# Three stacked graph attention layers on one Trainium2 core: score columns formed on VectorE, the first loads put in another order, ones multiplied on TensorE, and a new order for the first and last six turns

## The chip, the cores and the metric

The kernel runs on one core of one Trainium2 chip. The metric is the device time in microseconds (us) of one execution; of several executions the median is taken. The engines of the core are TensorE (PE in the rows), VectorE (DVE), ScalarE (ACT), GpSimd (POOL) and SyncE (SP), which here only issues transfers. Each engine works through its own instructions in order and waits for the others by semaphores.

## What is computed

There are 32 independent graphs of 256 nodes, with 256 float32 features each (`x`), and a 0/1 adjacency (`adj`, int32). Every layer projects the features, forms one score for each pair of nodes from two vectors of attention weights, masks it by the adjacency, takes a softmax, and averages the projected features with it:

```python
Wh = x @ W                                   # layer A: one head of 256
e = leaky_relu((Wh @ a1)[:, :, None] + (Wh @ a2)[:, None, :], 0.2)
h = elu(softmax(where(adj == 0, -1e9, e), axis=2) @ Wh)
x = layernorm(x + h)
# layer B: 4 heads of 128, softmax over the sources, mask adj > 0 or diagonal, + b1, elu
# layer C: input 512 wide, 1 head of 256, + b2
x = layernorm(x + layerC(elu(layerB(x))))
```

## The kernel before

One graph is one **turn** (32 in all, b0 to b5 for the first six, e6 to e1 for the last six). A turn passes through layer A (project, softmax, weigh, residual, layernorm), then B with four heads, then C. Several turns are in work at once, each at another stage. On every engine the order is written out by hand as three lists: `fill` (the first six turns), `body` (repeated 25 times, one full turn of work) and `drain` (the last six). Within a list a call such as `maxima(A, 0, 3, b0)` names layer, head or tile, the PSUM bank, and the turn.

A score of a projected row is the row times an attention vector. The kernel obtains it from the projection itself, by two more weight columns in front of W (columns 0 and 1 of `WA`, `WB`, `WC`), which hold W times the two attention vectors, scaled by 0.8 and -0.8. Before, TensorE makes these columns at the start: the transposed weights (`WTA`, `WTB`, `WTC`) are loaded as well, `scale_vectors` (L841) scales the vectors on VectorE, `score_products` (L1422) multiplies in pieces of two columns, and `score_columns` (L848) copies the sums into W. The first projection waits for that copy (`pe.wait_ge(A.s_wab, 1)` in `project_a`, L1457).

Weights of B and C are used as a rounded high part and a low part: `round_weights` on ScalarE waits for the score columns, and `split_weights` on VectorE for the rounding. The steps of one turn of layer A, which the first turn must pass through before B can begin, are: `project_a` (L1465, PE), `values` (ACT), `spread` (L1494, PE: scores laid out along rows), `maxima`, `top`, `logit`, `shift` (DVE), `exp` (ACT), `transpose_weights` (L1505, PE), `weights_copy` (ACT), `weigh` (L1513, PE), `inverse_sum` (L951, DVE), `norm_first`, `elu_exp_first` (ACT), `elu_first` (L963, DVE), `residual` (POOL), `stats`, `meanvar` (L1031, DVE), `rstd`, `normalise` (POOL), and `transpose_x1` (L1534, PE), with which the input of B is made. `column_sums` and `spread_b1` make the bias terms on TensorE, once. In C the last turn has the same steps, then `norm_last`, `stats`, `meanvar` and `normalise`, and a store.

`warm_up(b, count)` (L1455) multiplies a square of ones by itself count times; its result is not read. A float32 matmul of the program is two instructions in the trace.

Of the kernel before, what the change touches and what calls it, by code (L numbers as in the profile page):

```python
# [11 lines left out]
P = 128  # L12
# [37 lines left out]
def gat_kernel(nc, x, xT, adj, adjT, w0, w0T, w1, w1T, w2, w2T, vectors, biases, out):  # L50
# [13 lines left out]
    B = Layer("B", w1.shape[1] // P, P, D // P)  # L64
# [6 lines left out]
    with ctx:  # L71
# [15 lines left out]
        vec = sb("vec", [P, 2 * (D // P + B.H + D // P)])  # L87
# [4 lines left out]
        for L in LAYERS:  # L92
            L.W = sb("W" + L.name, [P, L.KT, L.H, L.F + 2])
            L.WT = sb("WT" + L.name, [P, L.H * L.F // P, L.KT * P])
# [11 lines left out]
        for L in LAYERS:  # L106
# [31 lines left out]
        s_cst, s_cst2, s_vec, s_rows, s_vecs, s_b1r, s_b1z, s_b1x, s_cs, s_b2 = (sem(n) for n in (  # L138
            "constants", "identity_made", "vectors_loaded", "biases_loaded", "vectors_scaled", "b1_spread", "b1_zeros", "b1_made",
            "column_sums", "b2_made"))  # L140
        for L in LAYERS:
            L.s_wld, L.s_wtld, L.s_wa, L.s_wab, L.s_round, L.s_split = (
                sem(k + L.name) for k in ("weights_loaded_", "weights_T_loaded_", "score_products_", "score_columns_",
                                          "weights_rounded_", "weights_split_"))
# [59 lines left out]
        def load_weights_T(eng, L):  # L204
            wT = w0T if L is A else w1T if L is B else w2T
            eng.dma_start(L.WT[:, :, :], wT.rearrange("(q p) k -> p q k", p=P)).then_inc(L.s_wtld, DMA)

        def load_vectors(eng):
            eng.dma_start(vec[:, :], vectors).then_inc(s_vec, DMA)
# [7 lines left out]
        def _(sp):  # L217
# [30 lines left out]
            def fill():  # L248
                b0, b1, b2, b3, b4, b5 = Turn(0), Turn(1), Turn(2), Turn(3), Turn(4), Turn(5)
                load_weights(sp, A)  # L250
                load_adj(b0)
                load_xT(b0)
                load_xT(b1)
                load_weights_T(sp, C)
                load_weights(sp, B)
                load_adj(b1)
                load_adjT(b0)
                load_residual(b0)
                load_weights(sp, C)
                load_adj(b2)  # L260
                load_adj(b3)
                load_residual(b1)
                load_xT(b2)
                load_adjT(b1)
                load_adjT(b2)
                load_residual(b2)
                load_adj(b4)
                load_adjT(b3)
                load_xT(b3)
                load_adjT(b4)  # L270
                load_xT(b4)
# [3 lines left out]
                store(b0)  # L275
                load_xT(b5)
                load_residual(b5)

# [8 lines left out]
            def drain():  # L287
                e6, e5, e4, e3, e2, e1 = Turn(NB - 6), Turn(NB - 5), Turn(NB - 4), Turn(NB - 3), Turn(NB - 2), Turn(NB - 1)
                load_xT(e1)
# [1516 lines left out]
```

## Time and profile before

| | |
|---|---|
| median of 3 runs | 669.05 us (668.47 to 672.19) |
| the profiled execution | 667.11 us, of which the profiled span is 665.2 us |
| TensorE busy | 637.9 us, 96% of the span |
| VectorE busy | 588.7 us, 88% |
| ScalarE busy | 482.0 us, 72% |
| GpSimd busy | 448.6 us, 67% |
| matmuls, weight loads | 4156 of each |

The page cuts the span into 40 slices. TensorE is at 90% or more of all slices but the first four and the last; the granted clock of TensorE is full in all but the last. Busy time is counted in microseconds of occupation, whatever the clock: a matmul at half the clock counts double. Where a row gives idle time in brackets, the name behind the arrow is what the engine had waited for.

### The profile page before, as it was taken

To read this page: it belongs to the slowest core of one execution; us is meant where nothing else is said; L and a number is where in the kernel's file an instruction comes from. 1 tells how busy PE (TensorE), PEld (TensorE's weight loads), DVE (VectorE), ACT (ScalarE), POOL (GpSimd) and SP (SyncE) were. 2 spreads that over 40 slices of the span, in tenths; PEclk is the share of its full clock that TensorE was granted. 3 is DMA by queue.
4 is the path that set the end of the run, shared out by engine and by line. 5 is a ranking of instruction groups with operands and counts; after the bars stand their busy time and mean duration, and the time that the engine had idled before them with its cause. 6 is when DMAs were issued, how large, how long until landed. Compare 5 with 4: busy or idle time off the path is not lost. (4 is left out here: it accounts for less than half of the span.)

```text
span 665.2 us, 17485 instructions
## 1 busy us (share of the span) xinstructions
PE 637.9 (96%) x4156; PEld 574.9 (86%) x4156; DVE 588.7 (88%) x2315; ACT 482.0 (72%) x1220; POOL 448.6 (67%) x811
## 2 busy tenths in 40 slices
PE   6979999999999999999999999999999999999993
PEld 5758899998999999999999989999999999988871
DVE  1488999999999999999999999999999999899953
ACT  1457887787778777777787777778877777687661
POOL 0247577777777777677777777777777777666762
PEclk9999999999999999999999999999999999999996
DMA  8311112222212222221122222211222222210001
GB/s 269 96 48 36 46 49 80 81 65 81 67 37 75 81 81 80 65 81 62 40 77 81 81 67 78 81 48 50 80 81 80 65 80 73 89 33 0 18 17 47
DMA packets 46693, 45.68 MB, mean 69 GB/s; under 512 B 2817, under 2 KB 46337, under 8 KB 46594
## 3 DMA queue, kind: packets, MB, share of 16 engines
q1 hardware_dynamic: 45648, 43.79, 20.8%
q8 instruction: 35, 0.57, 0.4%
q10 hardware_dynamic: 946, 0.80, 0.4%
q14 instruction: 64, 0.52, 0.3%
HBM read 36.19 MB, written 8.39 MB: 67 GB/s over the span
## 5 line engine op out<-in xcount | busy, mean ns | idle before, releaser
L378 POOL TENSOR_SCALAR probB<-probB,rdenB 128x256 f32<-128x256 f32 x256 | 124.7, 499 | 79.9 <-DVE rdenB L958 79.6
L558 ACT ACTIVATE probB<-probB,shiftB 128x256 f32<-128x256 f32 x256 | 127.1, 499 | 16.8 <-DVE shiftB L927 13.0
L1524 PE MATMUL PS<-probTB,VB 128*128 128x256 f32 x512 | 128.2, 382 | 0.9 <-ACT probTB L577 0.8
L941 DVE SCALAR_TENSOR_TENSOR probB<-PS,VB,gatedB 128x256 f32<-128x256 f32 x256 | 111.5, 478 | 1.8 <-issue 0.4
L389 POOL TENSOR_TENSOR inlC<-hidT,inhC 128x512 fp32r<-128x512 f32 x64 | 82.0, 1281 | 43.7 <-ACT inhC L622 43.6
L899 DVE CUSTOM_DVE_ANT_0 gatedB<-PS,gate_bc 128x256 f32<-128x256 f32 x256 | 93.8, 420 | 7.3 <-PE PS L1494 5.5
L1524 PEld LDWEIGHTS PS<-probTB,VB 128*128 128x128 f32 x512 | 89.3, 190 | 11.0 <-ACT probTB L577 2.1
L1480 PE MATMUL PS<-WhB,inhB 128*128 128x260 f32 x256 | 81.8, 319 | 1.4 <-DVE inlB L972 1.2
L577 ACT ACTIVATE probTB<-PS 128x512 f32<-128x512 f32 x128 | 72.9, 591 | 9.9 <-PE PS L1505 9.6
L360 POOL TENSOR_TENSOR y<-y,xres 128x512 f32<-128x512 f32 x32 | 41.1, 1286 | 52.4 <-DVE y L963 52.4
L1480 PE MATMUL PS<-WhC,inhC 128*128 128x258 f32 x256 | 75.4, 294 | 0.5 <-issue 0.4
L1505 PE MATMUL PS<-ident,probB 128*128 128x128 f32 x512 | 72.4, 273 | 1.4 <-POOL probB L378 1.4
L1480 PE MATMUL PS<-WlC,inhC 128*128 128x258 f32 x256 | 72.5, 283 | 0.0
L1480 PE MATMUL PS<-WhB,inlB 128*128 128x260 f32 x256 | 72.5, 283 | 0.0
L1480 PE MATMUL PS<-WlB,inhB 128*128 128x260 f32 x256 | 72.3, 282 | 0.0
L1480 PE MATMUL PS<-WhC,inlC 128*128 128x258 f32 x256 | 72.3, 282 | 0.0
L1513 PE MATMUL PS<-VC,probTC 128*128 128x257 f32 x256 | 67.3, 389 | 1.7 <-ACT probTC L577 1.7
L1465 PE MATMUL PS<-WA,xTin 128*128 128x258 f32 x256 | 65.4, 397 | 0.3 <-issue 0.3
L1513 PE MATMUL PS<-VA,probTA 128*128 128x257 f32 x256 | 64.7, 393 | 0.0
L1505 PEld LDWEIGHTS PS<-ident,probB 128*128 128x128 f32 x512 | 59.6, 141 | 5.5 <-issue 2.4
L611 ACT ACTIVATE ehid<-PS,minus 128x512 f32<-128x512 f32 x64 | 44.0, 687 | 28.1 <-issue 17.2
L987 DVE TENSOR_TENSOR VB<-PS,b1x 128x260 f32<-128x260 f32 x128 | 54.2, 426 | 10.6 <-PE PS L1480 9.2
(108 smaller groups left out, 1626.1 us busy)
## 6 DMA issues: line engine op xcount, KB each, us to landing
adj_in<-in_adj_dram SPq DMA_DIRECT2D x32, 256.0 KB, 4.3
xTin<-in_x_t_dram SPq DMA_DIRECT2D x32, 256.0 KB, 4.1
adjT_in<-in_adj_t_dram SPq DMA_DIRECT2D x32, 256.0 KB, 3.1
xres<-in_x_dram SPq DMA_DIRECT2D x32, 256.0 KB, 2.8
out_dram<-res SPq DMA_DIRECT2D x32, 256.0 KB, 2.1
WTC<-in_L_gnn_W_t_dram SPq DMA_DIRECT2D x1, 512.0 KB, 7.4
WTB<-in_L_gnn_W_t_dram ACTq DMA_DIRECT2D x1, 512.0 KB, 8.0
WB<-in_L_gnn_W_dram SPq DMA_DIRECT2D x2, 256.0 KB, 8.3
```

The lines of the kernel that those rows point to most:

```text
L378: last = pool.tensor_scalar(B.prob[h][:, k, :], B.prob[h][:, k, :], B.rden[:, k, h:h + 1], 1.0, ALU.mult, ALU.mult)
L389: pool.tensor_tensor(C.inl[:, s, :], hidT[:, s, :], C.inh[:, s, :].bitcast(F32), ALU.subtract)\
L558: last = nc.scalar.activation(L.prob[h][:, k, :], L.prob[h][:, k, :], ACT.Exp, bias=L.shift[:, k, h:h + 1], accum_out=den[:, k, h:h + 1] i ...
L577: nc.scalar.activation(L.probT[h][:, :, :], PS[b][:, :].rearrange("p (k n) -> p k n", k=NT), ACT.Copy)\
L899: last = nc.vector.tensor_tensor_reduce(out=L.gated[h][:, k, :], in0=PS[b][:, (h % 2) * N:(h % 2 + 1) * N], in1=gate[:, k, :], scale=0.25, ...
L941: last = nc.vector.scalar_tensor_tensor(out=L.prob[h][:, k, :], in0=PS[b][:, (h % 2) * N:(h % 2 + 1) * N], scalar=L.V[:, k, h, 1:2], in1=L ...
L987: nc.vector.tensor_tensor(B.V[:, tile, hs, :], PS[b][:, 0:2 * (B.F + 2)].rearrange("p (h f) -> p h f", h=2), b1x[:, hs, :], ALU.add).then_ ...
L1465: last = nc.tensor.matmul(PS[b][:, 0:D + 2], xTin[t.at % 2][:, k, tile * P:(tile + 1) * P], A.W[:, k, 0, :], start=(k == 0), stop=(k == A. ...
L1480: last = nc.tensor.matmul(PS[b][:, 0:n * (L.F + 2)], x_[:, k, tile * P:(tile + 1) * P], w_[:, k, n * g:n * (g + 1), :].rearrange("p h f -> ...
L1505: last = nc.tensor.transpose(PS[b][:, o:o + P], L.prob[h][:, q, k * P:(k + 1) * P], ident[:, :])
L1513: last = nc.tensor.matmul(PS[b][:, 0:L.F + 1], L.probT[0][:, k, u * P:(u + 1) * P], L.V[:, k, 0, 2:L.F + 3], start=(k == 0), stop=(k == NT ...
L1524: last = nc.tensor.matmul(PS[b][:, o:o + N], B.V[:, k, h, 2:B.F + 2], B.probT[h][:, k, :], start=(k == 0), stop=(k == NT - 1))
```

## The change

1. **Score columns.** `score_products`, `scale_vectors` and the loads of the transposed weights are gone. The attention vectors are loaded spread over all 128 partitions (`attA`, `attB`, `attC`), and VectorE multiplies each row of W by them and sums along the row, one instruction for each k, head and vector: 4 for A and 8 for C (256 columns), 16 for B (128 columns).
2. **Loads.** SyncE issues A's weights and the first xT, then waits until A's weights have landed, and issues the rest after that, adjacencies of b0 first. ScalarE issues A's vectors and the biases, waits for A's weights too, and issues the vectors of B and C. TensorE and ScalarE no longer wait for the identity at the start; the first `spread` does.
3. **Ones.** TensorE multiplies ones 11 times at the start (4 before), 6 times behind the first `spread`, 4 times behind the first `weigh`, and 12 times behind the last `spread`.
4. **Order.** `fill` and `drain` of all five engines are new lists of the same calls. `body` is the same.

```diff
+        def load_vectors(eng, L):
+            if L is A:
+                eng.dma_start(A.att[:, :, :], a0.rearrange("(j f) o -> j (f o)", j=2).partition_broadcast(P))\
+                    .then_inc(A.s_attld, DMA)
+            else:
+                for j, v in enumerate((asrc1, adst1) if L is B else (asrc2, adst2)):
+                    eng.dma_start(L.att[:, j, :], v.rearrange("h f -> (h f)").partition_broadcast(P))\
+                        .then_inc(L.s_attld, DMA)
...
                 load_weights(sp, A)
+                load_xT(b0)
+                sp.wait_ge(A.s_wld, DMA)
                 load_adj(b0)
-                load_xT(b0)
+                load_adjT(b0)
+                load_weights(sp, B)
+                load_weights(sp, C)
                 load_xT(b1)
-                load_weights_T(sp, C)
-                load_weights(sp, B)
                 load_adj(b1)
...
             def round_weights(L):
                 act.wait_ge(L.s_wld, (B.KT if L is B else 1) * DMA)
-                act.wait_ge(L.s_wab, 1)
+                act.wait_ge(L.s_wab, 2 * L.KT * L.H)
...
-                load_weights_T(act, A)
-                load_vectors(act)
+                load_vectors(act, A)
+                load_biases(act)
+                act.wait_ge(A.s_wld, DMA)
+                load_vectors(act, B)
+                load_vectors(act, C)
                 load_table()
...
+            def score_columns(L, k, heads):
+                dve.wait_ge(L.s_wld, (B.KT if L is B else 1) * DMA)
+                dve.wait_ge(L.s_attld, (1 if L is A else 2) * DMA)
+                for h in heads:
+                    for j in range(2):
+                        v = L.att[:, 1 - j if L is A else j, h * L.F:(h + 1) * L.F]
+                        if L.columns > 1:
+                            dve.wait_ge(L.s_wab, L.columns - 1)
+                        nc.vector.scalar_tensor_tensor(out=L.prod[:, j, :], in0=L.W[:, k, h, 2:L.F + 2],
+                                                       scalar=0.8 if j == 0 else -0.8, in1=v, op0=ALU.mult, op1=ALU.mult,
+                                                       accum_out=L.W[:, k, h, j:j + 1]).then_inc(L.s_wab, 1)
+                        L.columns += 1
...
                     if t.first:
                         pe.wait_ge(A.s_wld, DMA)
-                        pe.wait_ge(A.s_wab, 1)
+                        pe.wait_ge(A.s_wab, 2 * A.KT)
...
-                warm_up(7, 4)
-                score_products(A, 6)
-                project_a(1, 0, b0)
+                warm_up(0, 11)
+                project_a(0, 7, b0)
```

VectorE, the start of `fill`, before: two scaled vectors, then the softmax of b0, and the copies of C's and B's columns behind it.

```order
L874 TENSOR_SCALAR gate_a<-adj_in 128x512
L845 TENSOR_SCALAR vec<-vec 128x8 x2
L850 COPY WA<-PS 128x2x2
...
L927 SCALAR_TENSOR_TENSOR shiftA<-topA,amaxA 128x2
L951 RECIPROCAL rdenA<-PS 128x1 x2
L874 TENSOR_SCALAR gate_a<-adj_in 128x512
L850 COPY WC<-PS 128x4x2
L850 COPY WB<-PS 128x8x2
L883 TENSOR_SCALAR gate_bc<-adjT_in 128x512
L963 SCALAR_TENSOR_TENSOR y<-e,y 128x512
```

The same place now; `prod` takes the products, which nothing reads, and the sums go to W.

```order
L851 SCALAR_TENSOR_TENSOR prodA,WA<-WA,attA 128x256 x4
L877 TENSOR_SCALAR gate_a<-adj_in 128x512
...
L930 SCALAR_TENSOR_TENSOR shiftA<-topA,amaxA 128x2
L851 SCALAR_TENSOR_TENSOR prodB,WB<-WB,attB 128x128 x16
L851 SCALAR_TENSOR_TENSOR prodC,WC<-WC,attC 128x256 x2
L954 RECIPROCAL rdenA<-PS 128x1 x2
L877 TENSOR_SCALAR gate_a<-adj_in 128x512
L858 TENSOR_TENSOR WlB<-WB,WhB 128x1040
L851 SCALAR_TENSOR_TENSOR prodC,WC<-WC,attC 128x256 x2
L966 SCALAR_TENSOR_TENSOR y<-e,y 128x512
L851 SCALAR_TENSOR_TENSOR prodC,WC<-WC,attC 128x256 x4
L1024 BN_STATS statA<-y 128x6 x2
```

Eighteen products now stand between the first turn's shift and its reciprocals, two and the split of B's weights between these and its elu, and four between elu and statistics.

TensorE at the very start, before.

```order
L1455 MATMUL PS<-ones 128x128 x4
L1432 MATMUL PS<-vec,WTA 128x2 x4
L1465 MATMUL PS<-WA,xTin 128x258 x4
L1494 MATMUL PS<-ident,VA 128x128 x2
L1432 MATMUL PS<-vec,WTC 128x2 x8
L1505 MATMUL PS<-ident,probA 128x128 x4
L1465 MATMUL PS<-WA,xTin 128x258 x2
L1513 MATMUL PS<-VA,probTA 128x257 x4
L1432 MATMUL PS<-vec,WTB 128x2 x8
```

And now.

```order
L1450 MATMUL PS<-ones 128x128 x11
L1460 MATMUL PS<-WA,xTin 128x258 x4
L1491 MATMUL PS<-ident,VA 128x128 x2
L1450 MATMUL PS<-ones 128x128 x6
L1502 MATMUL PS<-ident,probA 128x128 x4
L1510 MATMUL PS<-VA,probTA 128x257 x4
L1450 MATMUL PS<-ones 128x128 x4
L1460 MATMUL PS<-WA,xTin 128x258 x2
```

The two-column products are gone, ones stand in their places, and the second turn's first projection has moved behind the first turn's weighing.

GpSimd, the last turns of `drain`, before: the correction of C's scores for the last turn (`VC<-VC,fix`) stands ahead of the layernorm of the turn before it.

```order
L389 TENSOR_TENSOR inlC<-hidT,inhC 128x512 x2
L336 TENSOR_SCALAR veC<-mvC 128x2
L337 TENSOR_SCALAR nmC<-mvC 128x2
L339 TENSOR_TENSOR rstdC<-veC,power 128x2
L352 TENSOR_SCALAR res<-y,nmC,rstdC 128x256 x2
L370 TENSOR_TENSOR x1b<-x,b2x 128x512
L399 TENSOR_SCALAR VC<-VC,fix 128x2
L336 TENSOR_SCALAR veC<-mvC 128x2
```

And now.

```order
L392 TENSOR_TENSOR inlC<-hidT,inhC 128x512
L355 TENSOR_SCALAR res<-y,nmC,rstdC 128x256 x2
L392 TENSOR_TENSOR inlC<-hidT,inhC 128x512
L339 TENSOR_SCALAR veC<-mvC 128x2
L340 TENSOR_SCALAR nmC<-mvC 128x2
L342 TENSOR_TENSOR rstdC<-veC,power 128x2
L355 TENSOR_SCALAR res<-y,nmC,rstdC 128x256 x2
L402 TENSOR_SCALAR VC<-VC,fix 128x2
```

One normalisation has moved between the two low parts that the last projection of C waits for, and the next turn's layernorm ahead of the last correction; on TensorE the 12 multiplications of ones stand there between the last spread and the transposes behind it.

## Rows read from the trace of the kernel before

**Rows 1.** The page's first part: busy us and share of the span.
```profile
PE 637.9 (96%) x4156; PEld 574.9 (86%) x4156; DVE 588.7 (88%) x2315; ACT 482.0 (72%) x1220; POOL 448.6 (67%) x811
```

**Rows 2.** Busy time by stretch: length, each engine, clock, DMA share, GB/s.
```profile
0.00:9.76 9.76, 3.92 (x16) 3.60 (x17) 0.90 (x5) 1.49 (x2) 1.07 (x11) 1.00 0.77 245
9.76:21.64 11.88, 11.40 (x37) 9.53 (x38) 1.84 (x8) 2.28 (x5) 0.00 (x0) 1.00 0.59 175
21.64:31.12 9.48, 8.06 (x41) 5.48 (x40) 5.39 (x21) 4.38 (x8) 3.48 (x7) 1.00 0.54 168
31.12:35.30 4.18, 4.18 (x19) 3.80 (x20) 2.88 (x6) 1.19 (x2) 2.51 (x4) 0.59 0.07 10
35.30:50.41 15.11, 10.41 (x61) 7.90 (x61) 13.44 (x51) 9.02 (x24) 6.72 (x13) 1.00 0.16 50
50.41:86.84 36.43, 36.35 (x240) 32.00 (x241) 32.00 (x127) 27.75 (x74) 23.99 (x42) 1.00 0.12 38
105.84:583.86 478.02, 477.27 (x3197) 437.88 (x3196) 454.90 (x1796) 372.48 (x946) 349.26 (x625) 1.00 0.23 71
640.00:665.20 25.20, 12.38 (x58) 8.99 (x56) 9.42 (x32) 6.04 (x13) 10.43 (x20) 0.76 0.12 42
```

**Rows 3.** The same of L1432 alone: length, PE, PEld, clock, DMA share, GB/s.
```profile
0.00:31.12 31.12, 7.12 (x40) 7.26 (x40) 1.00 0.63 195
```

**Rows 4.** Timeline of the start: start, duration, engine, line, instruction, idle before.
```profile
0.78 0.44 SPq L202 DMA_DIRECT2D WA<-in_L_gnn_W_dram  x1
2.05 2.05 PE L1455 MATMUL PS<-ones 128*128 128x128 f32 x8 [2.05 <-POOL ident L316]
7.29 0.24 DVE L845 TENSOR_SCALAR vec<-vec 128x8 f32<-128x8 f32 x2 [2.55 <-DMA vec<-in_vectors_dram]
...
9.76 3.78 PE L1465 MATMUL PS<-WA,xTin 128*128 128x258 f32 x8 [0.30 <-issue]
```

**Rows 5.** DMA issues of the first 60 us: size, median us to landing.
```profile
WB<-in_L_gnn_W_dram SPq DMA_DIRECT2D x2, 256.0 KB, 8.3
WC<-in_L_gnn_W_dram SPq DMA_DIRECT2D x1, 512.0 KB, 8.2
WA<-in_L_gnn_W_dram SPq DMA_DIRECT2D x1, 256.0 KB, 2.8
```

**Rows 6.** Timeline of the first turn's way to layer B; the last is turn b3's.
```profile
14.02 0.69 PE L1494 MATMUL PS<-ident,VA 128*128 128x128 f32 x2 [0.48 <-ACT VA L548]
17.88 1.08 PE L1505 MATMUL PS<-ident,probA 128*128 128x128 f32 x4
...
22.13 0.17 DVE L951 RECIPROCAL rdenA<-PS 128x1 f32<-128x1 f32 x1 [5.39 <-PE PS L1513]
25.10 0.69 DVE L963 SCALAR_TENSOR_TENSOR y<-e,y 128x512 f32<-128x512 f32 x1
28.22 0.25 DVE L1031 BATCH_NORM_AGGREGATE mvA<-statA 128x2 f32<-128x6 f32 x2
31.12 0.66 PE L1534 MATMUL PS<-ident,x 128*128 128x128 f32 x4 [0.89 <-POOL x L352]
...
86.84 0.61 PE L1534 MATMUL PS<-ident,x 128*128 128x128 f32 x4
```

**Rows 7.** Lines L963, L916 and L899 on VectorE: least, median and most ns.
```profile
L963 DVE SCALAR_TENSOR_TENSOR y<-e,y x32: 671/673/693, 25.1 to 612.5; 128x512 f32<-128x512 f32 x32
...
L916 DVE SCALAR_TENSOR_TENSOR topC<-amaxC,VC x32: 144/161/164, 68.2 to 650.5; 128x2 f32<-128x2 f32 x32
...
L899 DVE DVE_READ_ACCUMULATOR2_ANT amaxA<- x64: 81/83/88, 15.2 to 600.3; 128x1 f32 x64
```

**Rows 8.** Timeline of the end, behind the last projection of C.
```profile
649.16 0.40 PE L1494 MATMUL PS<-ident,VC 128*128 128x128 f32 x2 [0.57 <-ACT VC L548]
652.81 0.82 PE L1505 MATMUL PS<-ident,probC 128*128 128x128 f32 x4 [3.24 <-ACT probC L558]
654.40 3.77 PE L1513 MATMUL PS<-VC,probTC 128*128 128x257 f32 x8 [0.78 <-ACT probTC L577]
```

More of the change, by code:

```diff
@@ L1076, in fill @@
+                maxima(B, 1, 5, b0)
+                inverse_sum_head(3, b0)
+                top(B, 0, b0)
+                logit(B, 0, 5, b0)
+                shift(B, 0, b0)
+                elu_first(b1)
+                logit(B, 1, 5, b0)
+                inverse_sum_head(0, b0)
+                stats(A, b1)
+                meanvar(A, b1)
+                elu(1, 3, b0)
                 maxima(A, 0, 1, b2)
-                elu_first(b1)
+                make_gate_b(b2)
+                logit(A, 0, 1, b2)
@@ L1230, in drain @@
                 maxima(B, 3, 2, e4)
[L1231 to L1241 removed]
+                logit(B, 2, 2, e4)
+                top(B, 1, e4)
@@ L1242, in drain @@
+                elu(0, 6, e5)
+                shift(B, 1, e4)
+                values_b(1, 0, 0, e4)
+                make_gate_a(e2)
+                inverse_sum(A, 0, 5, e3)
+                values_b(0, 0, 4, e4)
+                logit(B, 3, 2, e4)
+                inverse_sum(A, 1, 3, e3)
+                maxima(B, 0, 1, e4)
+                inverse_sum_head(2, e4)
+                maxima(B, 1, 1, e4)
+                logit(B, 0, 1, e4)
+                top(B, 0, e4)
                 elu_first(e3)
-                maxima(B, 1, 5, e4)
@@ L1279, in drain @@
+                elu(0, 6, e4)
+                logit(B, 3, 3, e3)
+                shift(B, 1, e3)
+                values_b(1, 0, 7, e3)
+                values_b(0, 0, 2, e3)
+                inverse_sum(A, 0, 0, e2)
                 make_gate_a(e1)
-                logit(B, 3, 5, e3)
+                maxima(B, 1, 4, e3)
+                maxima(B, 0, 4, e3)
+                inverse_sum_head(2, e3)
+                top(B, 0, e3)
                 elu_first(e2)
-                shift(B, 1, e3)
-                values_b(1, 0, 0, e3)
@@ L1321, in drain @@
+                shift(C, 0, e4)
+                values_b(0, 1, 6, e2)
+                shift(A, 0, e1)
+                make_gate_b(e1)
+                elu(1, 2, e3)
+                values_b(1, 1, 7, e2)
+                maxima(B, 2, 7, e2)
+                logit(B, 2, 7, e2)
+                maxima(B, 3, 7, e2)
+                values_b(0, 0, 0, e2)
                 top(B, 1, e2)
+                values_b(1, 0, 3, e2)
+                elu(0, 4, e3)
                 shift(B, 1, e2)
-                elu_first(e1)
@@ L1400, in drain @@
+                shift(C, 0, e1)
+                inverse_sum(C, 0, 7, e1)
+                norm_last(0, 7, e1)
+                inverse_sum(C, 1, 0, e1)
+                norm_last(1, 0, e1)
                 stats(C, e1)
@@ L1488, in spread @@
                     take_bank(b, L.s_logit[2 * g:2 * g + 2], t)
+                    if t.first:
+                        pe.wait_ge(s_cst2, 1)
                     for tile in range(NT):
```

1149 lines of the change are left out of this document (538 added, 611 removed).

## The prediction

> **What bounds the kernel now.** I read the busy times first: TensorE is busy for 637.9 of 665.2 us [rows 1], and in the stretch of the full turns it is idle for 0.75 us of 478.0 [rows 2]. These turns stay as they are, so they can give nothing. What is left is the start and the end, read from the stretches [rows 2] and then from the timelines [rows 4, 6, 8].
>
> As the end of the start I take turn b3's transposes of x1 at 86.84 [rows 6]; TensorE has the same calls ahead of them in both lists, but for the score products and the ones. The start loses time in four ways:
> - the first projection runs at 9.76, behind a wait for the vectors (scaled from 7.29 on) and the products for A [rows 4];
> - the first turn's chain through layer A goes on to 31.12 [rows 6]. From 9.76 to 31.12 TensorE is idle for only 1.9 us [rows 2], but of its 23.4 busy us ahead of 31.12 the two-column products are 7.1 [rows 2, 3], and the durations show half the clock (1.2 GHz) up to about 21.6: four transposes take 1.08 us at 17.88 and 0.61 at 86.84 [rows 6]. The clock column says 1.00 there; the durations decide;
> - right after 31.12 there is a stretch at a granted clock of 0.59, 4.18 us of which about 3.4 lie at 1.2 GHz. That costs 1.7 us;
> - from 35.30 to 50.41 TensorE is idle for 4.7 us while VectorE is busy for 13.44 of 15.11 [rows 2].
>
> At the end, everything behind the last spread (649.16) is one chain of the last turn, 16.0 us to the end of the span. TensorE waits 3.24 us in it, and its last eight matmuls take 3.77 us [rows 8] in a stretch whose mean granted clock is 0.76 [rows 2].
>
> **The change part by part: the start.** I walk the first turn through the new lists, on the clock of the span.
>
> *First projection.* A's weights are issued at 0.78 and land 2.8 us later [rows 4, 5], so at 3.6. No row of before shows a load spread over the partitions; it lies between 3.6 (as A's weights) and 7.3 (when the small vector load was usable [rows 4]). I take 4.0, since it is now issued at once and little is in flight beside it. Then four products of 256 columns. The same instruction form on two SBUF operands takes 673 ns for 512 columns and 161 for 2 [rows 7], so 1.0 ns a column: 0.42 us for 256, 0.29 for 128. The read of the accumulator (83 ns) may lie beside the next one or come on top: 0.35 to 0.50, and 0.22 to 0.37. I take 0.43 and 0.29, with the operand form that is closest. The columns are ready at 4.0 + 1.7 = 5.7. TensorE is in its ones: 4 took 2.05 us [rows 4], so 11 take up to 5.6 from 1.5 on (the wait for the identity is gone), and the next matmul can start at about 6.6. So **6.6 for 9.76**; with vectors at 7.3 it is 9.0.
>
> *To the transposes.* From first projection to spread it took 4.26 us (9.76 to 14.02), of it 3.78 matmuls at half the clock. Eleven matmuls of full width and the projections then run back to back, so I take full clock (2.4 GHz) for most of it: 2.5 us, spread at 9.1 (at half the clock 10.9). Spread to transposes took 3.86, all of it the VectorE and ScalarE chain: now 3.6, transposes at 12.7. The six ones behind the spread take 1.7 us (3.1 at half the clock) inside that wait, so they are hidden either way. Gates of the first turn need adjacencies issued at about 3.7 and 4.2; at 2.8 us each, as A's weights, they are there before 9.1.
>
> *To the reciprocals.* The copy takes 0.6 and a latency; weighing starts at 13.95 and its first half could be inverted at 15.1. But VectorE's queue is in order, and between the shift (done at 11.5) and the reciprocals stand 16 products for B and 2 for C: 16 x 0.29 + 2 x 0.43 = 5.5. **The reciprocals come at 17.0** for 22.13 before, 1.9 later than the data (bounds 15.8 and 18.4). What is behind them waits as well: the rounding of B's weights, then the first turn's norms on ScalarE.
>
> *To x1.* Reciprocal to elu took 2.97 (22.13 to 25.10), and does so again, with the split of B's weights and two products inside it: elu at 20.0. Elu to the end of the aggregation took 3.37 (25.10 to 28.47); four products for C now fit beside the residual on GpSimd but for 0.1 to 0.4: 23.5. From there to x1 it took 2.65: **x1 at 26.1 for 31.12, 5.0 earlier**, with bounds of 23.5 and 29.5 from the ends above. Score products for C and B on TensorE lay beside this chain or delayed it; they are in the difference already. The bias matmuls fit into TensorE's idle time ahead of 26.1.
>
> *From x1 to b3.* Before, 31.12 to 86.84 held 50.9 us of busy time and 4.8 idle [rows 2]. The same calls at full clock are 49.2. The idle time does not shrink, since the first two turns must still go through VectorE, ScalarE and GpSimd one behind the other, and they start closer together with less TensorE work between them. Walking the heads of b0 I find waits of about 0.8, 1.9, 1.0, 0.7 and 1.7 us up to the second x1, and then little. I take 7.0 in all, between 4.8 (as before) and 10. The full turns are reached at 26.1 + 49.2 + 7.0 = 82.3 for 86.84: **4.5 us gained**; bounds about -1 and 9.
>
> **The end.** The same calls stand in other places. TensorE is idle for little ahead of the last projection, and that one is bound by the chain elu, high part, low part of the last turn, into which a normalisation on GpSimd is now put: I take 0, within 1.5 either way. Behind the last spread, 12 multiplications of ones take 2.7 us at full clock, inside the wait of 3.24 [rows 8]. If they hold the clock, the transposes take 0.6 for 0.82 and the weighing 1.9 for 3.77: **2.0 gained**. If the clock falls anyway, 0; if it had fallen before them, they take 5.4 and cost 2. The last correction of C's scores stands behind another turn's layernorm on GpSimd now; I find that one done about 1 us before it is wanted.
>
> **Sum.** -4.5 - 2.0 = -6.5: span 658.7 for 665.2, profiled execution 660.6 for 667.11. That execution was 1.9 us below the median of the runs, so against the median 669.05 - 6.5 = **662.5**.
>
> **A rule against the change.** L963 reads two float32 operands from SBUF at 1.0 ns a column [rows 7]. The Trainium skill ("Vector Engine (DVE) Microarchitecture Reference", section 7, Points that are easy to get wrong) says that this instruction with two SBUF sources that are not bf16 runs at half throughput, as both read ports are taken and none is left for reading back the accumulator. The row speaks against it, but that instruction accumulates nothing, and the new ones do. By the rule the time would be that of the first rival.
>
> **Rivals.**
> 1. *The sums cost double.* If a product that also sums takes 1.0 ns a column more, B's 16 take 2.1 us more, C's 8 take 2.1 and A's 4 delay the first projection by 0.1: x1 at 30.4, nearly all of the start's gain gone, 667.0. For it: no row shows this form. Against it: L963 at full rate. Chance 0.08.
> 2. *The clock does not follow.* Before, it rose only at about 21.6 with TensorE busy nearly throughout, and fell once behind a short wait. If it rises only behind the first projection (+1.9), falls for a stretch between x1 and the heads (+1.7), and is not held at the end (+2.0), the sum is 668.1; with half of it, 665.3. [...] Chance 0.12.
> 3. *Slower: VectorE's queue is blocked by landings.* It comes to B's products at 11.5 and stands there until B's and C's weights and vectors are in, the first turn behind it, one for one. B's weights took 8.3 us to land and C's 8.2 [rows 5], and the loads now start at about 3.7 with the vectors' copies beside them; I expect B at 10.5. Landing at 18 takes the whole 6.5; only from 21.4 is the kernel slower by more than 0.5%, at 672.5 and above. Chance 0.05.
>
> **Numbers.** A measurement tells about 0.5% from no change, 3.3 us. Forecast 0.75, with its own range of 658 to 665.5 from the bounds of x1, the idle time and the end; rival 1 0.08, rival 2 0.12 (half of it inside 0.5%), rival 3 0.05. Faster: 0.75 and some of rival 2, 0.79. Same: 0.16. Slower: 0.05. The range is 657.5 to 667.5.
>
> **What would show it.** The first projection at 6 to 7; score products at 0.29 and 0.43 us from start to start; reciprocals of b0 at 17, directly behind the last of 18 products; x1 at 26; TensorE idle for about 7 us from there to b3's x1 at 82; the last weighing in 1.9 us. It would be wrong if a landing is named in front of a product, if the four transposes of b0 still take 1.08, or if TensorE is idle for more than 10 us behind x1.

## The result, and the profile after

The changed kernel takes 674.6 us (median of 4 runs, 674.06 to 675.35); the kernel before took 669.2 beside it. The ratio is 1.0075, with a 95% interval of 1.0054 to 1.0096: slower by 5 us, where 6.5 us less were forecast. The profiled execution took 674.06 us, its span is 672.3.

The page's first part, for [rows 1]: TensorE is busy for 1.3 us more (two-column products out, ones in), VectorE for 11.3 us more.

```profile
PE 639.2 (95%) x4174; PEld 573.8 (85%) x4174; DVE 600.0 (89%) x2366; ACT 483.3 (72%) x1220; POOL 448.8 (67%) x811
```

Busy time by stretch, with the columns of [rows 2]. The stretches are cut at steps of the prediction: the first projection, x1 of the turns b0, b1, b3 and b4, x1 of the last three turns (e3, e2, e1), and the last spread of C.

```profile
0.00:6.81 6.81, 4.53 (x23) 4.37 (x23) 1.53 (x9) 0.00 (x0) 1.08 (x11) 1.00 0.44 126
6.81:29.40 22.59, 16.31 (x64) 11.49 (x64) 15.78 (x76) 8.09 (x14) 4.08 (x8) 0.85 0.70 206
29.40:47.08 17.68, 13.46 (x78) 10.35 (x79) 14.06 (x51) 10.20 (x28) 7.81 (x15) 1.00 0.23 76
47.08:86.15 39.07, 37.01 (x241) 31.76 (x241) 33.71 (x135) 28.30 (x73) 23.62 (x40) 1.00 0.14 42
86.15:105.69 19.54, 19.20 (x129) 17.56 (x129) 18.57 (x73) 14.28 (x38) 13.28 (x24) 1.00 0.19 61
105.69:583.98 478.29, 477.56 (x3195) 437.15 (x3194) 455.68 (x1800) 373.53 (x950) 350.77 (x625) 1.00 0.22 71
583.98:605.36 21.38, 20.53 (x133) 17.66 (x131) 19.75 (x76) 15.78 (x39) 13.87 (x26) 1.00 0.04 14
605.36:626.71 21.35, 19.31 (x127) 17.02 (x127) 17.69 (x71) 14.96 (x37) 14.68 (x30) 1.00 0.04 14
626.71:658.35 31.64, 25.63 (x156) 21.70 (x154) 19.02 (x68) 16.67 (x40) 17.18 (x30) 0.95 0.05 18
```

- **Start.** x1 of b0 stands at 29.40 for 31.12, x1 of b3 at 86.15 for 86.84 [rows 6]. Five microseconds had been forecast for the one, 4.5 for the other.
- **Full turns.** They are entered at 105.69 for 105.84 and left at 583.98 for 583.86 [rows 2]: in this pair of traces nothing is left of the start's gain. But traces of kernels with the same start lie up to 1.2 us apart at x1 of b4 (105.84 to 107.03 with the old start, 105.69 to 106.72 with the new one), so what the start is worth is read from the times (e2).
- **End.** From x1 of e3 to the last spread it is 74.4 us, for 65.3 before (583.86 to 649.16 [rows 2, 8]). TensorE waits 8.9 us in it, for 3.0 before (62.33 us busy of 65.30). This is where the kernel got slower. (The profiled execution of the kernel before lies 2 us below its median, so the spans differ by 7.1 us where the times differ by 5.)
- **Behind the last spread** it is 13.95 us to the end of the span for 16.04, as forecast.

VectorE at the start (timeline of after, as in [rows 4]). The products run one behind the other, and each wait names a landing.

```profile
5.24 0.42 DVE L851 SCALAR_TENSOR_TENSOR prodA<-WA,attA 128x256 f32<-128x256 f32 x1 [4.31 <-DMA WA<-in_L_gnn_W_dram]
5.59 0.08 DVE L851 DVE_READ_ACCUMULATOR prodA<-WA,attA 128x1 f32 x1
5.59 0.42 DVE L851 SCALAR_TENSOR_TENSOR prodA<-WA,attA 128x256 f32<-128x256 f32 x1
...
10.28 0.43 DVE L877 TENSOR_SCALAR gate_a<-adj_in 128x512 bf16<-128x512 int32 x1 [3.57 <-DMA adj_in<-in_adj_dram]
11.67 0.43 DVE L886 TENSOR_SCALAR gate_bc<-adjT_in 128x512 bf16<-128x512 int32 x1 [0.96 <-DMA adjT_in<-in_adj_t_dram]
12.01 0.42 DVE L902 CUSTOM_DVE_ANT_0 gatedA<-PS,gate_a 128x256 f32<-128x256 f32 x1
...
15.96 0.29 DVE L851 SCALAR_TENSOR_TENSOR prodB<-WB,attB 128x128 f32<-128x128 f32 x1 [2.08 <-DMA WB<-in_L_gnn_W_dram]
...
20.29 0.23 DVE L954 RECIPROCAL rdenA<-PS 128x1 f32<-128x1 f32 x2
```

TensorE in the same stretch:

```profile
6.81 1.98 PE L1460 MATMUL PS<-WA,xTin 128*128 128x258 f32 x8 [0.85 <-DVE prodA L851]
9.58 0.41 PE L1491 MATMUL PS<-ident,VA 128*128 128x128 f32 x2 [0.79 <-ACT VA L551]
9.82 1.50 PE L1450 MATMUL PS<-ones 128*128 128x128 f32 x12
14.94 0.66 PE L1502 MATMUL PS<-ident,probA 128*128 128x128 f32 x4 [3.62 <-ACT probA L561]
16.29 3.80 PE L1510 MATMUL PS<-VA,probTA 128*128 128x257 f32 x8 [0.69 <-ACT probTA L580]
...
29.40 0.66 PE L1531 MATMUL PS<-ident,x 128*128 128x128 f32 x4 [0.38 <-POOL x L355]
```

The first projection runs at full clock (2.4 GHz): eight matmuls in 1.98 us for 3.78. Behind the 3.62 us wait the clock falls: the weighing has a granted clock of 0.50 (1.2 GHz), and the same number of matmuls takes 3.80 us in it. TensorE had been busy with ones and the spread until 11.3 before that wait.

### The profile page after: what moved, and what is told of

The parts are those of the page before. It is cut to its first block and busy times, and to the rows that moved or that the text cites. A ratio compares the mean times of both kernels' runs of the same rounds, so it can differ in the third digit from the quotient of the medians.

```text
span 672.3 us, 17579 instructions
## 1 busy us (share of the span) xinstructions
PE 639.2 (95%) x4174; PEld 573.8 (85%) x4174; DVE 600.0 (89%) x2366; ACT 483.3 (72%) x1220; POOL 448.8 (67%) x811
## 5 line engine op out<-in xcount | busy, mean ns | idle before, releaser
L381 POOL TENSOR_SCALAR probB<-probB,rdenB 128x256 f32<-128x256 f32 x256 | 126.1, 506 | 71.7 <-DVE rdenB L961 71.4
L1510 PE MATMUL PS<-VA,probTA 128*128 128x257 f32 x256 | 66.1, 399 | 0.9 <-ACT probTA L580 0.9
L1510 PE MATMUL PS<-VC,probTC 128*128 128x257 f32 x256 | 65.5, 381 | 1.1 <-ACT probTC L580 1.1
L990 DVE TENSOR_TENSOR VB<-PS,b1x 128x260 f32<-128x260 f32 x128 | 54.3, 425 | 10.3 <-PE PS L1475 9.2
L1460 PE MATMUL PS<-WA,xTin 128*128 128x258 f32 x256 | 62.5, 382 | 0.8 <-DVE prodA L851 0.8
```

What stands on the lines that cost most here:

```text
L381: last = pool.tensor_scalar(B.prob[h][:, k, :], B.prob[h][:, k, :], B.rden[:, k, h:h + 1], 1.0, ALU.mult, ALU.mult)
L990: nc.vector.tensor_tensor(B.V[:, tile, hs, :], PS[b][:, 0:2 * (B.F + 2)].rearrange("p (h f) -> p h f", h=2), b1x[:, hs, :], ALU.add).then_ ...
L1460: last = nc.tensor.matmul(PS[b][:, 0:D + 2], xTin[t.at % 2][:, k, tile * P:(tile + 1) * P], A.W[:, k, 0, :], start=(k == 0), stop=(k == A. ...
L1510: last = nc.tensor.matmul(PS[b][:, 0:L.F + 1], L.probT[0][:, k, u * P:(u + 1) * P], L.V[:, k, 0, 2:L.F + 3], start=(k == 0), stop=(k == NT ...
```

## The experiments

### Which part is slower: the last six turns, the start, or the ones

Three kernels build the change from its parts. e1: the kernel before with the new lists of the last six turns, ones included. e2: the changed kernel with the old lists of the last six turns, without ones. e3: the kernel before, with

```diff
                 spread(C, 0, 2, e1)
+                warm_up(0, 12)
                 transpose_weights(C, 0, 5, e1)
```

(`warm_up` of e1 and e3 also waits for its bank to be free, as in the changed kernel.)

> The kernel before, with the changed kernel's lists for the last six turns on all five engines (its 12 multiplications of ones behind the last spread among them); start and full turns as before. Theory D, the loss comes from the new order of the last six turns: in the changed kernel the last spread came 9.2 us later (658.35 for 649.16) and the chain behind it was 2.1 shorter, and 0.6 of that was already there at the last full turn, so 6.5 us slower than before, about 675.5. Theory F, the start's work on VectorE leaves the full turns and the end behind: within 1.5 us of before, about 669.

Measured: 674.1 us, ratio 1.0092 (1.0062 to 1.0123).

> The changed kernel with the lists of before for the last six turns; the new start (score columns on VectorE, held loads, ones, order) stays. Theory D: the start's net is what turn b3 shows, 0.2 to 0.7 us earlier than before, and the end is the old one: 668.5 to 669.5. Theory F: as slow as the changed kernel or nearly, 672 to 675.

Measured: 667.4 us, ratio 0.9983 (0.9972 to 0.9994).

> The kernel before with one addition: TensorE multiplies ones 12 times behind the last spread. If they hold TensorE's clock at its high level over the last turn's chain, as in the changed kernel where the last eight matmuls took 1.97 us for 3.77, 2.0 us faster than before, about 667.2. If the clock in the changed kernel was high for another reason (its own last stretch), no difference, 669.2.

Measured: 666.0 us, ratio 0.9961 (0.9936 to 0.9986). The end of e3's TensorE timeline, for [rows 8]:

```profile
649.77 0.40 PE L1495 MATMUL PS<-ident,VC 128*128 128x128 f32 x2 [0.57 <-ACT VC L548]
653.42 0.63 PE L1506 MATMUL PS<-ident,probC 128*128 128x128 f32 x4 [0.56 <-ACT probC L558]
654.82 1.97 PE L1514 MATMUL PS<-VC,probTC 128*128 128x257 f32 x8 [0.78 <-ACT probTC L577]
```

The ones fill the wait, and the last weighing takes 1.97 us for 3.77. So the start gives 0.2% (1.1 us, with an interval of 0.4 to 1.9), the ones give 0.4% (2.4 us by the medians), and the new order of the last six turns costs the ratio of e1 to e3, 1.0092/0.9961 = 1.013, some 8.8 us. The start with the ones and the old order, e5, is the better of both:

> The new start with the old last six turns, plus the 12 multiplications of ones behind the last spread. If the parts simply add: -0.2% of the start and -2.4 us of the ones, so about 665.3 us (664.5 to 666) against 668.3 before. If the start's small gain is absorbed at the end, it is the ones alone, 666 to 667.

Measured: 665.3 us, ratio 0.9949 (0.9932 to 0.9966). The parts add. Against it the changed kernel is 1.0075/0.9949 = 1.0127 slower, 8.4 us, again the order of the last six turns alone.

### Why the start gave so little: landings and a cold clock

e4 is the changed kernel without the two waits for A's weights in front of the later loads.

> The changed kernel with the two waits for A's weights taken away, on SyncE and on ScalarE, so that all first loads are issued at once in the same order. Theory H, the held loads cost time in the start: adjacencies (at 10.28 and 11.67) and B's weights (15.96) land about 2 us earlier while A's weights land later by less than 1, and the first turn's x1 (29.40) comes 1 to 2 us earlier. Whether that reaches the end: if the first turns' order gives it back as it did the other gains, below 1 us, about 674; if the start's gain passes on, 673 or less.

Measured: 673.4 us, ratio 1.0066 (1.0040 to 1.0093); x1 of b0 came 0.13 us earlier. That expectation fell. VectorE's timeline of e4:

```profile
9.06 0.43 DVE L875 TENSOR_SCALAR gate_a<-adj_in 128x512 bf16<-128x512 int32 x1 [1.94 <-DMA adj_in<-in_adj_dram]
11.47 0.43 DVE L884 TENSOR_SCALAR gate_bc<-adjT_in 128x512 bf16<-128x512 int32 x1 [1.98 <-DMA adjT_in<-in_adj_t_dram]
```

The first adjacency is there 1.2 us earlier, but the transposed one only 0.2, and its gate stands in front of the maxima although layer A of b0 does not read it. And the weighing again took 3.79 us on the half clock. B's weights did come in time: the products for B ran from 13.61 on, without a wait, for 15.96. The reciprocals then had to wait for the slow weighing:

```profile
18.51 0.17 DVE L952 RECIPROCAL rdenA<-PS 128x1 f32<-128x1 f32 x1 [0.53 <-PE PS L1508]
20.22 0.17 DVE L952 RECIPROCAL rdenA<-PS 128x1 f32<-128x1 f32 x1 [1.54 <-PE PS L1508]
```

In the changed kernel the weighing ends at 20.09 and the last product at 20.29. Two limits end together there, and taking away one of them gains nothing. The next kernel, on top of e5, takes away both:

```diff
                 load_xT(b0)
-                sp.wait_ge(A.s_wld, DMA)
...
                 make_gate_a(b0)
-                make_gate_b(b0)
...
                 shift(A, 0, b0)
+                make_gate_b(b0)
...
                 spread(A, 0, 6, b0)
-                warm_up(0, 2)
-                warm_up(1, 2)
-                warm_up(7, 2)
+                warm_up(0, 4)
+                warm_up(1, 4)
+                warm_up(7, 4)
```

(ScalarE's wait for A's weights is gone too.)

> e5 with three edits in the start: no wait for A's weights ahead of the later loads, the gate of the transposed adjacency behind the first shift instead of ahead of the maxima, and 12 instead of 6 multiplications of ones behind the first spread. Theory (the start was late by the landing of the transposed adjacency and by the clock that fell in the 3.6 us wait): maxima at about 10 for 12.0, transposes at 12.8 to 13.5 for 14.9, the weighing of b0 in about 2 us for 3.8, reciprocals of b0 directly behind the products at 16.5 to 17.5, x1 of b0 at 26 to 27 for 29.4, x1 of b3 1 to 3 us earlier than 86.15, and the time 662.5 to 664.5. Rival (what the first turn gains is given back in the next turns, where TensorE waits for VectorE and ScalarE): x1 of b0 at 26 to 27, but x1 of b3 within 0.5 of 86.15 and the time equal to that of e5. Second rival (the cold clock has other reasons): the weighing still takes 3.8 us, x1 of b0 at 28 or later.

Measured: 663.7 us, ratio 0.9926 (0.9897 to 0.9955), faster than the kernel before and than the changed one. TensorE's timeline:

```profile
10.08 0.40 PE L1489 MATMUL PS<-ident,VA 128*128 128x128 f32 x2 [0.57 <-ACT VA L550]
10.32 2.84 PE L1448 MATMUL PS<-ones 128*128 128x128 f32 x24
13.56 0.66 PE L1500 MATMUL PS<-ident,probA 128*128 128x128 f32 x4 [0.40 <-ACT probA L560]
14.90 2.00 PE L1508 MATMUL PS<-VA,probTA 128*128 128x257 f32 x8 [0.69 <-ACT probTA L579]
...
26.99 0.66 PE L1529 MATMUL PS<-ident,x 128*128 128x128 f32 x4 [0.71 <-POOL x L354]
```

With a wait of 0.40 instead of 3.62 us the clock stayed full, and the weighing took 2.00. The reciprocals stand at 17.89, directly behind the products, for 20.29. The three edits were made together: the earlier maxima made the wait shorter too (spread to transposes 3.48 us, for 5.36), so what each edit is worth is not shown. x1 of b0 came at 26.99, x1 of b3 at 84.2 instead of e5's 86.4, and the difference is still there in the last turn: 2.7 us won at the first x1 are 2.2 at the last spread. So what the start wins is mostly kept, and the rival that it is given back falls. It did not win enough in the changed kernel.

### Is it TensorE's work that sets the end, and is it one late call

In the old order the transposes of the last turn's weights of layer A stand at 604.75, directly behind x1 of e2. In the new order they stand at 612.01, and from there to the last spread it takes about as long as before. First before, then after:

```profile
604.75 0.63 PE L1505 MATMUL PS<-ident,probA 128*128 128x128 f32 x4
```

```profile
612.01 0.60 PE L1502 MATMUL PS<-ident,probA 128*128 128x128 f32 x4
```

Two kernels halve ten calls behind that place which do not feed the last turn:

```diff
-                weigh(C, 1, 6, e4)
+                weigh_k0(C, 1, 6, e4)
```

(and so on: `weigh` of C for e4, e3, e2 and the four `weigh_head` of e2, each with the first half of its sum only; e9 in the new order, e10 in the old one).

> The changed kernel; in its last six turns ten calls behind the last turn's layer A transposes multiply only the first half of their rows, so part of the aggregation is left out: the weighing of C for the three turns before the last, and the four heads of B for the turn before the last. None of them feeds the last turn. That is 20 matmul instructions pairs less, about 4.3 us of TensorE work (0.43 us a half). Theory L (behind the last turn's layer A the end is set by the last turn's chain through all engines, not by the amount of TensorE's work): the last spread of C moves by less than 1.5 us from 658.35, and the time is 671.5 to 673.5. Rival W (TensorE's work sets the end in the new order too): it moves by 3.5 to 4.5 us, to 654 to 655, and the time is 669 to 670.5.

Measured: 676.1 us, ratio 1.0097 (1.0067 to 1.0127).

> The same ten calls halved in the kernel before (again a part of the aggregation is left out). Theory L as I hold it: the old order is bound by TensorE's work until some 10 us before the last spread, which moves by 2 to 4.4 us from 649.16, and the time is 664.5 to 666.5; it gains at least 1 us more than the new order does. Rival W: both gain the same. Rival that both are bound by the last turn's chain: less than 1.5 us here too, 667 to 668.3.

Measured: 669.8 us, ratio 1.0009 (0.9991 to 1.0027). Neither got faster than the kernel that it was made from; e9 lies above both of its ranges. The stretch from those transposes to the last spread, columns as above, in this order: before, e10, after, e9.

```profile
604.75:649.16 44.41, 42.24 (x276) 36.45 (x277) 34.34 (x133) 31.95 (x83) 29.19 (x53) 1.00 0.05 16
```

```profile
606.50:650.70 44.20, 38.73 (x258) 32.51 (x256) 34.17 (x133) 31.68 (x83) 29.24 (x54) 1.00 0.05 17
```

```profile
612.01:658.35 46.34, 38.49 (x236) 32.90 (x234) 31.84 (x121) 26.54 (x67) 27.93 (x48) 0.96 0.05 18
```

```profile
612.50:659.88 47.38, 35.45 (x217) 30.10 (x214) 31.45 (x121) 26.70 (x67) 27.96 (x49) 0.93 0.07 23
```

In the old order TensorE is busy for 42.24 of 44.41 us, 95%. With 3.5 us of that gone the stretch is 0.2 us shorter (e10's trace runs 1.2 us later from the first turns on, and its window starts and ends 0.2 us late): the 95% were work that fitted into a time set by something else, not the bound. My own expectation for the old order (2 to 4.4 us) fell. In the new order the test is less clean: with 3.0 us less of busy time the stretch became 1.0 us longer, at a lower mean clock (0.93 for 0.96). The Trainium skill ("Perfetto Trace Analysis", Identifying the Most-Contended Engine) says to find the engine with the highest occupancy and to optimise it first; TensorE's distance to its roofline it judges by the busy share of the weight loads and not by that of the matmuls. By either share TensorE comes first in this stretch (42.24 and 36.45 us of 44.41, VectorE 34.34), and e10 shows that less work on it gained nothing.

From those transposes to the last spread it is 44 to 46 us in the kernel before, e10 and the changed kernel, and they start 7.3 us later in the new one. So the late start looked like the cause. Two kernels moved the last turn's layer A forward in the new order, and one moved it back in the old one:

```diff
                 weigh_head(3, 2, e3)
+                transpose_weights(A, 0, 3, e1)
...
-                transpose_weights(A, 0, 2, e1)
```

(e7 and e12, TensorE; with `shift`, `exp`, `weights_copy`, `weigh`, the norms, elu, residual and layernorm of that turn on the other engines. In e8 the same calls stand later: transposes behind `transpose_weights(B, 1, 4, e3)`.)

> The changed kernel, with only the last turn's layer A (shift, exp, transposes, weighing, norms, residual, layernorm) moved forward by some calls in its last six turns; every other call keeps its place. Theory L (the last turn's chain is what ends last, and it starts late): the exp of the last turn's layer A ends at 604 to 606 for 610.2, its transposes at 606 to 608 for 612, the last spread of C at 651 to 655 for 658.4, and the time 667.5 to 671. Rival O (the end is late by the order of what stands behind it, C's stages of the turns before and the normalisation between the two low parts): the exp comes as early, but the last spread stays at 657 or later and the time at 673 or more.

Measured: 679.2 us, ratio 1.0149 (1.0122 to 1.0176).

> As e7 (only the last turn's layer A moved forward in the new order), but with its elu on VectorE behind the scores of the turn before, where e7 put it ahead of them, and with its weighing ahead of that turn's spread. In e7 VectorE stood 1.3 us for ScalarE at that elu and the scores of the turn before came 5 us later than in the changed kernel. Theory L: with that stall gone, the last turn's transposed weights come at about 608 for 614.7 and its x1 at 618 to 622 for 626.7, the last spread at 651 to 655, the time 667.5 to 671. Rival (the places between are taken, and each call moved forward delays one that another turn waits for): x1 of the last turn not before 625, time 673 or more.

Measured: 678.6 us, ratio 1.0133 (1.0100 to 1.0165).

> The kernel before, with only the last turn's layer A (exp, transposes, weighing, norms, elu) moved back by some calls, 3 to 5 us of TensorE's work; every other call keeps its place. Theory L: the last turn's transposed weights come 3.5 to 5.5 us later than at 606.0, the last spread of C 2.5 to 5 us later than at 649.2, TensorE's idle time ahead of it grows by as much, and the time is 670.5 to 673.5. Rival O: other calls fill the place, the last spread stays within 1 us and the time at 668 to 669.3.

Measured: 678.0 us, ratio 1.0135 (1.0111 to 1.0160). e8 moved in the expected direction, but too far: the last turn's transposes stand 5.5 us later behind x1 of e2 (6.1 us behind it, for 0.6), and the time is 9 us longer. e7 and e12 had the exp and the transposes of the last turn early, as wanted (606.54 and 607.27 for 612.01), and were slower by 4 to 5 us than the changed kernel. From those transposes to the last spread it is 57.2 us in e7, 56.7 in e12 and 48.3 in e8, for 46.3 in the changed kernel: what is gained at the beginning of the last turn is lost behind it. In e7 one sees a part of what it cost: VectorE stands at the last turn's elu for ScalarE, the scores of the turn before are late behind it, and TensorE waits for these, for a bank.

```profile
617.82 1.25 DVE L966 SCALAR_TENSOR_TENSOR y<-e,y 128x512 f32<-128x512 f32 x1 [1.31 <-ACT e L597]
```

```profile
621.62 0.36 PE L1475 MATMUL PS<-WhC,inhC 128*128 128x258 f32 x1 [3.19 <-DVE probB L944]
```

In e12, with that elu moved behind the scores, x1 of the last turn came at 631.57, 4.9 us later than in the changed kernel (626.71). So a late start of the last turn is not a cause that can be mended by itself, and the last turn's own steps are not all that sets the end: how the calls of the other turns stand between them counts as well.

e11 tests the one term of the end that the prediction named:

```diff
                 low_c(1, e1)
-                normalise(C, e3)
                 low_c(0, e1)
+                normalise(C, e3)
```

> The changed kernel, with GpSimd's normalisation of another turn moved from between the two low parts of the last projection to behind both. It is the one term of the end that the prediction named. By the trace the second low part could start at about 652.95 and starts at 653.33, so 0.4 us earlier: last spread at 657.9 to 658.0 for 658.35, time 673 to 674.3. If this normalisation were the cause of the late end, the spread would come 1.1 us earlier or more.

Measured: 674.6 us, ratio 1.0084 (1.0054 to 1.0113): no difference in the time. From x1 of e1 to the last spread e11's trace has 31.24 us for 31.64, the 0.4 us that were expected. Behind it the moved call takes more than that back. GpSimd is done with the last correction of C's scores at 661.2 (658.7 in the changed kernel), and VectorE waits for it:

```profile
661.41 0.16 DVE L919 SCALAR_TENSOR_TENSOR topC<-amaxC,VC 128x2 f32<-128x2 f32 x1 [1.27 <-POOL VC L402]
```

TensorE then waits 1.81 us behind its ones, for 0.56, and the last weighing takes 3.65 us for 1.97. (That execution, 677.5 us, was the slowest of the four; the others took 674.4 to 674.6.) So by this trace the normalisation between the low parts costs 0.4 us of the 8.4 to 8.8, and no more.

### In which stretch the new order loses

Four kernels cut the lists of all engines at one place and take one order ahead of it, the other behind it. All have the new start and 12 ones. The ratio is 0.9949 for the old order throughout (e5) and 1.0075 for the new one throughout.

> The last six turns in the new order up to the transposes of x1 of the third turn from the end (e3, at about 584), and in the old order from there on, on all engines; new start, 12 ones behind the last spread. A bank of PSUM was chosen anew for each tile behind the cut, the one that comes free first. With the old order throughout this kernel took 665.3, with the new one throughout (the changed kernel) 674.1 to 674.6. If the loss arises behind e3: 664.5 to 667; if ahead of it: 672 to 675.

> The same with the cut at the transposes of x1 of e2 (about 605). Theory L2 (the loss arises between x1 of e2 and x1 of e1, where the transposes of the last turn's weights moved back): 665.5 to 668. Rival E (the new order is late already at e2, with work on other turns that the old order had done by then): 671 to 675.

> The same with the cut at the transposes of x1 of e1, the last turn (626.7 in the new order). Theory L2: 671 to 675. Rival (the loss arises behind x1 of e1, in the order of C's steps): 665 to 668.

> The other way round: the old order up to the transposes of x1 of e2, the new one from there on. Theory L2: 671 to 675. Rival E: 665.3 to 668.

| kernel | new order | us | ratio (95%) | step |
|---|---|---|---|---|
| e5 | nowhere | 665.3 | 0.9949 (0.9932 to 0.9966) | |
| h1 | up to x1 of e3 | 666.6 | 0.9952 (0.9934 to 0.9970) | +0.2 us |
| h2 | up to x1 of e2 | 667.3 | 0.9966 (0.9955 to 0.9977) | +0.9 us |
| h3 | up to x1 of e1 | 671.0 | 1.0005 (0.9986 to 1.0023) | +2.6 us |
| after | throughout | 674.6 | 1.0075 (1.0054 to 1.0096) | +4.7 us |
| h4 | only behind x1 of e2 | 676.6 | 1.0107 (1.0078 to 1.0137) | |

The steps are differences of the ratios times 669. Each ratio is known to within about 1 us, so the first two steps are not clear of noise and the last two are. h4 lies above its range. The last spread in h2, h3 and h4 (TensorE's timelines, 658.35 in the changed kernel):

```profile
651.46 0.40 PE L1491 MATMUL PS<-ident,VC 128*128 128x128 f32 x2 [0.57 <-ACT VC L551]
```

```profile
655.20 0.40 PE L1491 MATMUL PS<-ident,VC 128*128 128x128 f32 x2 [0.57 <-ACT VC L551]
```

```profile
660.03 0.40 PE L1491 MATMUL PS<-ident,VC 128*128 128x128 f32 x2 [0.52 <-issue]
```

So most of the loss arises behind x1 of e2, in two pieces: 2.6 to 3.7 us between x1 of e2 and x1 of e1, and 3.2 to 4.7 us behind x1 of e1. Theory L2, which put it all in the first piece, holds for less than half of it. h2 also shows that the last turn's late start is a thing of order, not of lateness carried in: with the new order up to x1 of e2 and the old one behind, the end is only 1.1 us late. h4 shows the reverse: a good order ahead does not save the new one behind it. Which single exchange of calls costs what within the two pieces stays open.

In the second piece the clock fell as well, in the trace of after. TensorE's timeline at a head of the last turn, behind a wait:

```profile
643.53 1.08 PE L1502 MATMUL PS<-ident,probB 128*128 128x128 f32 x4 [1.36 <-issue]
```

Four transposes take 1.08 us for 0.6, and the half clock lasts until about 647. This is not what makes the new order slow. e1 has the same lists there and the same wait of 1.36 us, at the full clock throughout. First after, then e1, with the columns of [rows 2]:

```profile
640.00:650.00 10.00, 8.07 (x43) 6.76 (x42) 6.19 (x24) 6.18 (x17) 4.09 (x11) 0.83 0.00 0
```

```profile
640.00:650.00 10.00, 7.49 (x49) 6.21 (x48) 6.74 (x27) 6.74 (x18) 4.63 (x12) 1.00 0.00 0
```

From x1 of e1 to the last spread it is 31.64 us in after and 30.80 in e1, and 30.83 in h4, whose clock is full too. So the fall of the clock costs 0.8 us in this trace, and the loss is there without it.

## Why the prediction was wrong, point by point

| step | predicted | after |
|---|---|---|
| first projection | 6.6 | 6.81 |
| spread | 9.1 | 9.58 |
| transposes of the weights | 12.7 | 14.94 |
| reciprocals | 17.0 | 20.29 |
| elu | 20.0 | 22.60 |
| x1 of b0 | 26.1 | 29.40 |
| x1 of b3 | 82.3 | 86.15 |
| behind the last spread | -2.0 | -2.1 |
| order of the last six turns | 0, within 1.5 | +8.4 (e5) to +8.8 (e1, e3) |

**The step that failed is the last line.** The prediction said "The same calls stand in other places. TensorE is idle for little ahead of the last projection", and took 0. The row behind that reading was true (42.24 busy of 44.41), the inference was not: e10 shows that TensorE's busy time there is filling, so a small idle time does not mean that the order is worth nothing. What the order did cost is shown from both sides: the new lists put into the kernel before (e1 against e3) take 8.8 us more, the old ones put into the changed kernel (e5) 8.4 us less, and the cuts put 2.6 to 3.7 us of it between x1 of e2 and x1 of e1 and 3.2 to 4.7 behind. How the order does it is argued and not shown: a step of the last turns passes through four in-order engines and can be held up by every call of another turn put in front of one of its own, and the diff moved dozens. Which exchanges did it stays open. With the sign unknown, the range needed several microseconds on this term, where it had 1.5. The rival that would have caught it (the last turn is held up by an order in which its calls stand later) was not among the three.

**The start was right in mechanism and mis-sized.** The first projection came close by luck: the forecast had the columns ready at 5.7 and TensorE in its ones until 6.6 (its own terms, 1.5 and 5.6, add up to 7.1); in fact the ones ended at 5.96 and TensorE waited for the columns. The products cost what was taken, or less: 0.34 from start to start for 256 columns (0.43 taken), 0.21 for 128 (0.29). Rival 1 is refuted, and with it, for this form, the rule of the Trainium skill ("Vector Engine (DVE) Microarchitecture Reference", section 7) that was weighed against the change; the accumulator is read in 0.08 us beside the next product. The sizes that were off are landings. A's weights took 4.4 us for the 2.8 taken from the row of before, with their vectors, spread over the partitions, in flight beside them (4.1); the adjacencies were usable at 10.3 and 11.7 for "before 9.1", and the gate of the second stood in front of the maxima, which the prediction did not price; B's weights came at 15.96 for 10.5. Of the 2.2 us by which the transposes came later than forecast, 1.4 are that gate (the maxima start at 12.01, and could have started at 10.6 behind the first one), 0.5 the later spread, and the rest the first adjacency. At the reciprocals another 1.1 is lost: VectorE stood 2.1 us for B's weights ahead of the products (rival 3's mechanism, at a small dose), and the quicker products gave half of that back. From there to the elu it went 0.7 us quicker than taken (2.3 for 3.0), and from elu to x1 0.7 slower, the product held up beside the residual (last section). With the gate moved, the loads released and the clock held, x1 of b0 comes at 26.99 (e6): 2.4 of the 3.3 us that it was late.

**Rival 2 was half true.** The clock rose earlier than before, and fell again in the first turn's wait, where the prediction had costed the six ones as "hidden either way". Hidden they were, and too few: the weighing took 3.80 us for 2.00 in e6. In the changed kernel this lay beside VectorE's products, which ended no earlier; in e4, where they did, it took all that was gained. At the end the ones held the clock in the traces of after and e3, but not in that of e11, where a wait of 1.81 us followed them.

**From x1 to b3** 56.2 us had been forecast (49.2 of calls, 7.0 idle) and 56.75 were measured, so the start's -4.5 became -0.7 almost only by the 3.3 us at x1. At the next turn, b4, 0.15 of these 0.7 is left in this pair of traces; the new order brings b1's and b2's exps of layer A 2.1 and 4.3 us later than the old one, and from b3 to b4 it takes 19.54 us for 19.00, 0.34 of them idle where TensorE was not idle before. The prediction took all that is gained at b3 as kept; that was not checked by any row.

**The ones behind the last spread** gave 2.1 us in the profile and 2.4 by medians (e3): right, in size and in mechanism.

In sum: -1.1 of the start, -2.4 of the ones, and +8.8 of the order make +5.3, for 5.0 measured.

## What to carry to other kernels

In the last turns of a pipeline a busy TensorE says little: ask what the end would do if a tenth of its work were gone, and if the answer is not clear from the trace, give a reordering there several microseconds both ways. A gate or copy that an early step does not read must not stand in front of it in an in-order queue. A landing taken from the old trace does not carry over when the loads beside it change: A's weights took 2.8 us before, 4.4 in the changed kernel, and 4.8 and 5.1 with all loads issued at once (e4, e6). Where two limits end together, as the weighing and the products do here, take away both before judging either. Ones in a wait held the clock here where they left little of it (0.56 us in e3, 0.40 in e6) and did not where they left 3.62 (after) or 1.81 (e11).

## What the runs showed of the hardware

A product of two float32 operands from SBUF that stood beside a GpSimd operation with two SBUF operands took 1.48 us instead of 0.42, until just behind that operation's end (24.74). After, VectorE's and GpSimd's timelines:

```profile
23.54 1.48 DVE L851 SCALAR_TENSOR_TENSOR prodC<-WC,attC 128x256 f32<-128x256 f32 x1
```

```profile
23.37 1.37 POOL L363 TENSOR_TENSOR y<-y,xres 128x512 f32<-128x512 f32 x1 [10.57 <-DVE y L966]
```

The Trainium skill ("SBUF — State Buffer", SBUF: two separate sides) says that such a pair shares an exclusive lock and the later one is blocked until the first is done; this row agrees. e4 and e6 show the same 1.48 us at the same place. The prediction let four products of C run beside the residual on GpSimd but for 0.1 to 0.4 us; the one product took 1.1 us more, and from elu to the end of the aggregation it was 4.1 us for 3.4.
